# Delta-rule stage: f32 products replaced by products of f16 pairs, single buffers for the decayed blocks and decay rows

## The reference, cut to what matters

```python
def step(state, inp):
    q_t, k_t, v_t, g_t, b_t = inp
    state = state * jnp.exp(g_t)[..., None, None]
    kv_mem = jnp.einsum('bhkv,bhk->bhv', state, k_t)
    delta = (v_t - kv_mem) * b_t[..., None]
    state = state + k_t[..., None] * delta[..., None, :]
    out = jnp.einsum('bhkv,bhk->bhv', state, q_t)
    return (state, out)
```

## Time and profile before

| | before |
|---|---|
| median of 3 runs | 3533.2 us (3532.31 to 3538.77) |
| the profiled execution's own time | 3529.42 us |
| its span, first to last instruction | 3527.7 us |
| mean granted clock of PE over the span | 0.954 |
| PE, PEld busy | 3090.6 us (88%), 2170.7 us (62%) |
| DVE, ACT, POOL busy | 2636.8 us (75%), 2127.8 us (60%), 1516.7 us (43%) |
| first and last second-chunk cast (one for each unit) | 886.2 us, 3175.2 us |

### The profile page before, as it was taken

The page is one execution under the profiler, slowest core; times in us unless marked ns, Lnnn a source line. Parts: engine busy times, 40 slices in busy tenths (PEclk is TensorE's granted clock), DMA queues, the critical chain, the costliest instruction groups (busy, mean ns, idle before and its releaser), DMA issues. The chain is left out here.

```text
span 3527.7 us, 82159 instructions
## 1 busy us (share of the span) xinstructions
PE 3090.6 (88%) x29280; PEld 2170.7 (62%) x29280; DVE 2636.8 (75%) x4740; ACT 2127.8 (60%) x5446; POOL 1516.7 (43%) x1853
## 2 busy tenths in 40 slices
PE   6999788347999999999999999999999999983285
PEld 4666565235777676776767767677676777762142
DVE  3444389874888877888778887788877888776875
ACT  4444410135777777777777777777777777763553
POOL 1111177224555454555545555455554555530000
PEclk9999999778999999999999999999999999996698
DMA  4000011001101011010110101101011010101101
GB/s 191 13 13 1 9 39 42 24 21 46 37 20 38 20 34 42 20 38 20 38 38 20 38 20 42 34 20 38 20 44 33 20 37 20 44 8 63 80 1 48
DMA packets 43229, 120.67 MB, mean 34 GB/s; under 512 B 5824, under 2 KB 10048, under 8 KB 39488
## 3 DMA queue, kind: packets, MB, share of 16 engines
q1 hardware_dynamic: 42816, 115.30, 10.6%
HBM read 110.75 MB, written 4.54 MB: 33 GB/s over the span
## 5 line engine op out<-in xcount | busy, mean ns | idle before, releaser
L2020 DVE TENSOR_TENSOR delta_Pb<-delta_bank,delta_lev 128x512 f16<-128x512 f32 x448 | 311.2, 695 | 196.1 <-PE delta_bank L2350 194.6
L1590 POOL TENSOR_SCALAR_AFFINE_SELECT delta_LA<-delta_LA 128x512 f32<-128x512 f32 x128 | 81.2, 635 | 807.0 <-DVE delta_LA L2049 797.6
L2012 DVE SCALAR_TENSOR_TENSOR delta_F<-delta_bank,delta_cw,delta_F 128x510 f32<-128x510 f32 (+1 forms) x512 | 381.2, 745 | 62.4 <-ACT delta_far L1828 50.1
L2324 PE MATMUL delta_bank<-delta_xh,delta_qkvh 128*128 128x512 f16 x1024 | 390.6, 381 | 4.6 <-DVE delta_qkvl L1985 3.1
L2324 PE MATMUL delta_bank<-delta_xl,delta_qkvh 128*128 128x512 f16 x1024 | 390.4, 381 | 0.0
L2324 PE MATMUL delta_bank<-delta_xh,delta_qkvl 128*128 128x512 f16 x1024 | 390.3, 381 | 0.0
L1610 POOL TENSOR_TENSOR delta_F<-delta_F,delta_far 128x506 f32<-128x506 f32 x256 | 277.6, 1084 | 207.0 <-DVE delta_F L2012 207.0
L1822 ACT ACTIVATE delta_F<-delta_bank,delta_cw 128x512 f32<-128x512 f32 x256 | 178.1, 696 | 270.5 <-PE delta_bank L2324 270.2
L2037 DVE CAST delta_XT<-delta_bank 128x512 f16<-128x512 f32 x384 | 263.2, 686 | 78.0 <-PE delta_bank L2369 77.3
L2309 PE MATMUL delta_bank<-delta_zh,delta_xh 128*128 128x256 f16 x1024 | 279.0, 272 | 0.6 <-ACT delta_gz L1850 0.6
L2309 PE MATMUL delta_bank<-delta_zl,delta_xh 128*128 128x256 f16 x1024 | 278.8, 272 | 0.0
(11 more groups left out here) (352 smaller groups left out, 9302.3 us busy)
## 6 DMA issues: line engine op xcount, KB each, us to landing
delta_Gb<-g_rows SPq DMA_DIRECT2D x66, 512.0 KB, 5.4
delta_st_qkv<-in_Wqkv SPq DMA_DIRECT2D x17, 1024.0 KB, 8.7
conv_T<-filters SPq DMA_DIRECT2D x32, 256.0 KB, 3.1
delta_st_zo<-in_Wz SPq DMA_DIRECT2D x16, 512.0 KB, 9.3
delta_st_zo<-in_Wout SPq DMA_DIRECT2D x16, 512.0 KB, 6.4
ffn_ahead_W<-in_W SPq DMA_DIRECT2D x2, 4096.0 KB, 16.7
conv_ahead_C<-in_ctx_rev SPq DMA_DIRECT2D x1, 6144.0 KB, 26.5
attn_xt<-in_xT SPq DMA_DIRECT2D x8, 512.0 KB, 4.2
```

Source lines behind the costliest of these rows:

```text
L2012: ve.scalar_tensor_tensor(dst, src, cw_tap(i, 3 - lag), dst, ALU.mult, ALU.add)\
L2020: ve.tensor_tensor(left(Pb[:, lvl, :, :], lvl), comp(bank[5], lvl), bc(lev[:, lvl, :].rearrange("p (n s) -> p n s", s=1 << lvl), 1, 8), AL ...
L2324: ins = te.matmul(bk[:, :], ww[:, QKV[job], kc, :], xx[:, kc, tok:tok + 512], start=(m == 0), stop=(m == 11))
```

## The change

L00, L11, L10, A00, A10 and A11 now lie in one f32 buffer `LA` of 6 x 128 columns for each q. A00, A10, A11 and L10 are split into f16 pairs: the high parts by ACT (`split_high`, four copies of 128x512 in a turn), the low parts by POOL (`split_low`, four subtractions of 128x512). `Ah` and `Al` have two buffers by parity, `Bh` and `Bl` (L10) one. `W` is gone: the first answer stays in `W16`, now one for each chunk, and `refined` casts the correction to `Wl16`. Each of the sixteen f32 matmuls of a unit becomes three f16 ones (`split_product`). `decayed_j0` no longer waits for `o` of two units earlier, but for `ll` and `alo` of the unit before. `Gb` has one buffer, loaded three units ahead of unit 0 and not four. Two aliases of the prologue move to `gz`. The core of the diff:

```diff
-        Gb = sb("Gb", [P, 2, 2, 512])
+        Gb = sb("Gb", [P, 2, 512])
-        LA = sb("LA", [P, 2, 4, 2, 384])
+        LA = sb("LA", [P, 4, 768])
+        Ah, Al = sb("Ah", [P, 2, 3, 4, P], F16), sb("Al", [P, 2, 3, 4, P], F16)
+        Bh, Bl = sb("Bh", [P, 4, P], F16), sb("Bl", [P, 4, P], F16)
-        W, W16 = sb("W", [P, 2, 4, P]), sb("W16", [P, 4, P], F16)
+        W16, Wl16 = sb("W16", [P, 2, 4, P], F16), sb("Wl16", [P, 2, 4, P], F16)
+        L00, L10, A00, A10, A11 = 128, 256, 384, 512, 640
+        split_from = (A00, A10, A11, L10)
+        def split_to(n, u, part):
+            return (Bh, Bl)[part][:, :, :] if n == 3 else (Ah, Al)[part][:, u % 2, n, :, :]
...
@@ def turn of @block.sync @@
-                    if it.has(4):
-                        load_g(it.u(4), it.kh(4))
+                    if it.has(3):
+                        load_g(it.u(3), it.kh(3))
...
@@ def turn of @block.gpsimd @@
+                def split_low(n):
+                    after("ahi", n + 1, 1)
+                    if n < 3:
+                        after("o", 2, -1)
+                    else:
+                        after("sv", 4, 0)
+                    by_sequencer()
+                    gp.tensor_tensor(split_to(n, it.u(1), 1), LA[:, :, split_from[n]:split_from[n] + P],
+                                     split_to(n, it.u(1), 0), ALU.subtract).then_inc(g["alo"].sem, 1)
+
                 if it.has(1):
+                    split_low(0)
                     after("v", 2, 1)
                     after("sv", 1, 0)
                     by_sequencer()
                     gp.tensor_copy(V16[:, :, :], values[it.u(1) % 2][:, :, 0, :]).then_inc(g["v16"].sem, 1)
                 if it.has(2):
                     conv_far("v1")
+                if it.has(1):
+                    split_low(1)
...
                 if it.has(1):
                     low_L(0)
                     low_L(1)
+                    split_low(2)
+                    split_low(3)
...
@@ def turn of @block.scalar @@
+                def split_high(n):
+
+                    if not it.has(1):
+                        return
+                    after("la", 8, 1)
+                    if n < 3:
+                        after("o", 2, -1)
+                    else:
+                        after("sv", 4, 0)
+                    sc.activation(split_to(n, it.u(1), 0), LA[:, :, split_from[n]:split_from[n] + P], ACT.Copy)\
+                        .then_inc(g["ahi"].sem, 1)
...
                 gate(0)
+                split_high(0)
+                split_high(1)
+                split_high(2)
                 conv_tap("v1")
                 level_x(1, 1)
                 next_qkv(0)
                 next_qkv(1)
+                split_high(3)
                 first_answer(1)
...
@@ def turn of @block.vector @@
-                    after("o", 2, -1)
+                    after("ll", 2, 0)
+                    after("alo", 4, 0)
...
                     after("sv", 3 + 4 * k, 0)
-                    after("u0", k + 1, 0)
-                    ve.tensor_tensor(W[:, k, :, :], W16[:, :, :], heads(bank[2]), ALU.add).then_inc(g["w"].sem, 1)
+                    ve.tensor_copy(flat(Wl16[:, k, :, :]), bank[2][:, :]).then_inc(g["w"].sem, 1)
...
@@ def turn of @block.tensor @@
+                def split_product(out, q, n, k, start, stop):
+                    high, low = (split_to(n, it.u(0), part)[:, q, :] for part in (0, 1))
+                    te.matmul(out, high, W16[:, k, q, :], start=start, stop=False)
+                    te.matmul(out, high, Wl16[:, k, q, :], start=False, stop=False)
+                    return te.matmul(out, low, W16[:, k, q, :], start=False, stop=stop)
...
-                            last = te.matmul(out, LA[:, it.u(0) % 2, q, 0, P:2 * P], W[:, 0, q, :], start=True,
-                                             stop=True)
+                            last = split_product(out, q, 3, 0, True, True)
...
-                        te.matmul(out, LA[:, it.u(0) % 2, q, 1, P:2 * P], W[:, 0, q, :], start=True, stop=False)
-                        last = te.matmul(out, LA[:, it.u(0) % 2, q, 1, 2 * P:3 * P], W[:, 1, q, :], start=False,
-                                         stop=True)
+                        split_product(out, q, 1, 0, True, False)
+                        last = split_product(out, q, 2, 1, False, True)
```

More of the change, by code:

```diff
@@ L1380, in delta_stage @@
             sv=7, u0=2, r=2, w=2, t16=1, t2=1, o=2,
-            so=8, rr=1, lr=1, rn0=1, rn=3, ogs=8, og=2, ct=2, ch=2, cl=2,
+            ahi=4, alo=4, so=8, rr=1, lr=1, rn0=1, rn=3, ogs=8, og=2, ct=2, ch=2, cl=2,
         ).items():
             g[name] = counter(name, per)
-        g_load = [counter(f"g_load{i}", 1, 16) for i in range(2)]
+        g_load = counter("g_load", 1, 16)
         w_load = {n: counter(f"load_{n}", 1, 16) for n in ("qkv", "z", "o", "c")}
@@ L1396, in delta_stage @@
         pro_g = counter("pro_gstore", 0, 16)
-        wba = LA[:, 1, 0, :, :].rearrange("p a b -> p (a b)")[:, 0:256].rearrange("p (k c) -> p k c", k=KC)
+        wba = LA[:, 0, 0:256].rearrange("p (k c) -> p k c", k=KC)
         wbah = Pb[:, 0, 0:2, :].rearrange("p a b -> p (a b)").rearrange("p (k c) -> p k c", k=KC)
         wbal = Pb[:, 0, 2:4, :].rearrange("p a b -> p (a b)").rearrange("p (k c) -> p k c", k=KC)
-        dtr = LA[:, 1, 1, 0, 0:32]
-        nal = LA[:, 1, 1, 0, 32:64]
-        al0 = LA[:, 1, 1, 0, 64:96]
+        dtr = LA[:, 1, 0:32]
+        nal = LA[:, 1, 32:64]
+        al0 = LA[:, 1, 64:96]
         full = lambda t: t.rearrange("p a b -> p (a b)").rearrange("p (a b) -> p a b", b=NVH)
@@ L1410, in delta_stage @@
         gg = full(V[:, 1, 4:8, :])
-        lnb = full(W[:, 0, :, :])
+        lnb = gz[:, 0:2, :].rearrange("p a b -> p (a b)").rearrange("p (a b) -> p a b", b=NVH)
         tri = EL[:, 0, 0:128]
-        GT = W[0:32, :, :, :].rearrange("p a b c -> p (a b c)")
+        GT = gz[0:32, :, :].rearrange("p a b -> p (a b)")
         def left(t, lvl):
@@ L1513, in _ @@
             turns(nc, ENG.SP, turn)
-            for par in range(2):
-                sp.wait_ge(g_load[par].sem, g_load[par].at(NU // 2 + 1))
+            sp.wait_ge(g_load.sem, g_load.at(NU + 1))
             sp.wait_ge(w_load["qkv"].sem, w_load["qkv"].at(NKH + 1))
@@ L1586, in unit_diagonal @@
                     par = it.u(1) % 2
-                    diag = LA[:, par, :, 0, 256 * c:256 * c + P]
+                    diag = LA[:, :, L00 - P * c:L00 - P * c + P]
                     after("la", 4 + 4 * c, 1)
@@ L1793, in first_answer @@
                     after("sv", 1 + 4 * k, 0)
-                    sc.activation(flat(W16[:, :, :]), bank[2][:, :], ACT.Copy).then_inc(g["u0"].sem, 1)
+                    sc.activation(flat(W16[:, k, :, :]), bank[2][:, :], ACT.Copy).then_inc(g["u0"].sem, 1)
+                def split_high(n):
[8 more added lines that the diff above has]
+                        .then_inc(g["ahi"].sem, 1)
                 def token_major(b_):
@@ L2467, in times_L @@
                     if blk == 1:
+                        after("u0", 1, 0)
                         after("w", 1, 0)
+                        after("alo", 4, 0)
                     else:
@@ L2474, in times_L @@
                         if blk == 1:
-                            last = te.matmul(out, LA[:, it.u(0) % 2, q, 0, P:2 * P], W[:, 0, q, :], start=True,
-                                             stop=True)
-                        else:
-                            te.matmul(out, Lt16[:, it.u(0) % 2, 2 * q + k, :], W16[:, q, :], start=True, stop=False)
-                            last = te.matmul(out, Ll16[:, 2 * q + k, :], W16[:, q, :], start=False, stop=True)
+                            last = split_product(out, q, 3, 0, True, True)
+                        else:
+                            te.matmul(out, Lt16[:, it.u(0) % 2, 2 * q + k, :], W16[:, k, q, :], start=True, stop=False)
+                            last = te.matmul(out, Ll16[:, 2 * q + k, :], W16[:, k, q, :], start=False, stop=True)
                     last.then_inc(g["sv"].sem, 1)
@@ L2486, in output_first @@
                     for q in range(4):
-                        last = te.matmul(bank[OUT[0]][:, q * P:(q + 1) * P], LA[:, it.u(0) % 2, q, 1, 0:P],
-                                         W[:, 0, q, :], start=True, stop=True)
+                        last = split_product(bank[OUT[0]][:, q * P:(q + 1) * P], q, 0, 0, True, True)
                     last.then_inc(g["o"].sem, 1)
```

18 lines of the change are left out of this document (9 added, 9 removed).

## The result

The changed kernel takes 3510.4 us, the median of four runs (3504.9 to 3513.3), beside 3535.7 (3532.3 to 3538.8, four runs) for the kernel before: ratio 0.9931, interval 0.9912 to 0.9949. It is faster by 25 us. The forecast was 42 faster, 3491 us; 3510 lies in the stated range, 3458 to 3529, but outside the 3480 to 3502 of the case that was held likeliest.

A forecast was written before the change was run, and what follows sets the result against it. PE was taken to bound the delta stage (1978 of 2000 us busy). Plain turns -48 and loaded turns +6 gave -42 us: 3529.4 to 3487, forecast as a 3491 us median, range 3458 to 3529.

The forecast's parts named there:

- the case that was held likeliest: Whole kernel: the main forecast, 3491 us for a median, own range 3480 to 3502, chance 0.50.
- The products' lengths: PE's L10 W0, A00 W0 and `output_second` go from 0.97, 0.95, 1.87 to 0.67, 0.67, 1.34 us.
- L10 W0 and the wait behind it: PE keeps 0.30 us of this product, plus 0.18 waiting for DVE's f16 cast, which beats POOL by 0.24.
- rival 1: PE's wait for w2 doesn't bind, so plain turns are 1.3 us shorter: 70 us saved, 3463; chance 0.11.
- A00 W0's 0.28 lost to the wait for w2: PE's shorter A00 W0 gains nothing: it waits 0.4 us for DVE's `add_out(0, -1)` instead of about 0.1.
- ACT's and POOL's additions cost nothing in plain turns: ACT's three copies (1.84 us) fit a 1.95 us hole; POOL's 4.6 us of subtractions is covered.
- DVE never waited for `alo`: `decayed_j0(0)`'s new wait on DVE has over two us left; DVE waiting there would make the forecast wrong.
- stretched DVE steps in plain turns: Sign against the forecast: DVE's other steps with two inputs in SBUF stretched in plain turns; no size given.
- Loaded turns later at `level_a(3, 1)`: In 16 loaded turns w2 starts 0.6 to 1.2 us later; each turn +0.4 (+0.1 to +0.7), together +6 us.
- rival 2: DVE's cast loses the port to POOL in 16 to 32 plain turns, worth 0 each: 3507 to 3523; chance 0.20.
- rival 3: DVE's cast loses the port everywhere; plain turns give 0.0, loaded ones lose 11 us: 3544; chance 0.11.
- the sum itself: 48 plain turns at 1.01 us saved, 16 loaded at 0.4 added: -48 + 6 = -42 us.

The follow-up runs named there:

- experiment 6: Changed kernel with 60 turns in one iteration (no jump), plus five overwritten f16 matmuls in `output_first`: 3468.3 us, 1.4 more than without them.
- experiment 4: Changed kernel with its loop body lengthened to 60 turns in one iteration, so no jump back: 3466.9 us, ratio 0.9817 to the kernel before.
- experiment 5: Kernel before with 60 turns in one iteration, so no jump back: 3514.0 us, ratio 0.9953 to the kernel before.
- experiment 1: Changed kernel with 32 f16 matmuls (64 instructions) put ahead of PE's loop, results overwritten: 3491.7 us, one run.
- experiment 2: Changed kernel with 64 f16 matmuls (128 instructions) put ahead of PE's loop, results overwritten: 3490.3 us, one run.
- experiment 10: Changed kernel with 96 matmuls (192 instructions) put ahead of PE's loop: 3495.7 us, one run.
- experiment 7: Changed kernel without jumps, with DVE's `add_out(0, -1)` moved ahead of `level_p(3, 1)` and `refined(1)`: 3451.0 us, ratio 0.9772 to the kernel before.
- experiment 11: Changed kernel without jumps, DVE's `add_out(0, -1)` early and POOL's `split_low(0)` behind its v1 convolution: 3448.2 us, ratio 0.9755 to the kernel before.

## Why the prediction was right and wrong

- **The products' lengths** (0.67, 0.67, 1.34): right, to the hundredth.
- **L10 W0 and the wait behind it, 0.30 + 0.18:** right in kind, too small. In plain turns the cast won the port with the margin worked out, ended 0.29 behind POOL, and the wait went. But it was longer than its bracket. The earlier trace rows show 0.18 at 1724.15; the start before it was 1723.57, and eight such matmuls take 0.24, so PE stood for 0.34. The bracket counts from the modelled end of a matmul. With 0.34 a plain turn loses 1.17, and 1.20 were measured. That is a term of the sum too small by 48 x 0.16 = 8 us, and the sign named for rival 1, plain turns shorter by 1.3, was nearly met by it (1.20), though rival 1's reason is wrong.
- **A00 W0's 0.28 lost to the wait for w2:** right (0.38 of waiting in each plain turn; experiment 6). Rival 1 falls.
- **ACT's and POOL's additions cost nothing in plain turns:** right. ACT's three copies fit in the hole and 0.39 of it is left:

```profile
1710.77 1.68 ACT L1826 ACTIVATE delta_Ah<-delta_LA 128x512 f16<-128x512 f32 x3
1712.83 0.69 ACT L1855 ACTIVATE delta_F<-delta_bank,delta_cw 128x512 f32<-128x512 f32 x1 [0.39 <-PE delta_bank L2362]
```

DVE never waited for `alo`. `low_L` began at 1719.31 without a gap behind `split_low(1)`, and the z weights' low parts on DVE went from 1.28 to 2.79 us for two beside POOL, with nobody waiting for them. The prediction had named stretched DVE steps in plain turns as a sign against it; here they came, in one plain turn of four, and cost nothing.
- **Loaded turns later at `level_a(3, 1)`:** right, +0.3 against +0.4, by fours of turns (3 x 1.20 - 3.3). Job w2 starts 8.87 us behind the cast, where it was 8.07 in loaded turns of before (8.40 in the one of the earlier trace rows, which has the jump): 0.80 later, inside the 0.6 to 1.2 forecast. The chain is the one foretold, POOL to ACT to PE:

```profile
1787.51 1.17 POOL L1662 TENSOR_TENSOR delta_Al<-delta_LA,delta_Ah 128x512 f16<-128x512 f32 x1
1788.61 0.62 POOL L1670 CAST delta_V<-delta_V 128x512 f16<-128x512 f32 x1
1789.17 1.53 POOL L1616 TENSOR_TENSOR delta_F<-delta_F,delta_far 128x506 f32<-128x506 f32 x1
```

```profile
1790.74 0.63 ACT L1870 ACTIVATE delta_F<-delta_F 128x512 f32<-128x512 f32 x1 [1.53 <-POOL delta_F L1616]
...
1791.80 0.58 ACT L1808 ACTIVATE delta_Xi<-delta_bank 128x512 f16<-128x512 f32 x1
```

```profile
1792.43 0.41 PE L2388 MATMUL delta_bank<-delta_Xi,delta_Lt 128*128 128x64 f16 x8 [1.11 <-ACT delta_Xi L1808]
```

- **Rivals 2 and 3, the port lost:** it was lost in four turns of 64, those behind the jumps, where rival 2 had it in 16 to 32; the median of the casts is 0.54 us. Such a turn was worth 0.1 us (36.07 to 35.96), near rival 2's 0. The time, 3510, stands in rival 2's own range, 3507 to 3523, but the lost casts are 4 x 0.9 = 4 us of it; most of the way there came from the jumps. That the time is in the stated range is owed in part to luck: the range was wide for rivals 1 and 2, and had nothing in it for what happened.
- **What failed is the sum itself.** It was made of plain and loaded turns, 48 and 16, and had no term for the four turns in which PE jumps back. What the runs show in its place is +7.2 us each, +29 us. Without the jumps the sum of -42 would have stood beside -49 (from the fours of turns) or -47 (experiments 4 and 5). The diff doesn't touch the jump, but it changes the number of PE's instructions in each turn, and with it the loop's place and length (which of the two counted here was not separated: the place alone moved the idle time by 2.2 us in the one kernel and by 3.4 in the other, and no place tried brought the kernel after down to 1.3); and PE's waits of before have four gaps of 1.1 to 1.6 us marked `issue`, which the forecast didn't read.

That the idle time is the fetching of instructions is argued from the times in the traces, not shown by an experiment. The profile has DMA queues of kind "instruction". On one of them, q8, packets of 16 KB come every 14 us or so. The DMA view of after from 1800.5 to 1800.8 has one:

```profile
q8 instruction: 1, 0.02, 28.2%
```

It starts at 1800.64, and 28.2% of 16 engines' 0.3 us is 1.35 us, so it landed at 1802.0; PE goes on at 1803.39, 1.4 later. It is so at every idle time over half a us at or behind a jump, in all kernels with jumps, 34 in number: the last packet of q8 landed 1.2 to 2.4 us before PE's next instruction. The length goes with when that packet starts. In the kernel after it starts 2.5 to 3.3 us after PE has stopped (5.3 us idle), in the kernel before 1.4 to 1.5 ahead of the stop (1.3 idle), and with the loop moved (experiments 1 and 2, and the first idle time of 10) it starts 0.2 to 0.8 ahead (1.9 to 3.3 idle). Three idle times without a jump have such a packet too, of 0.5 us in experiment 4 and of 1.2 in 7 and 11. That q8 is PE's own queue is inferred from this. One `issue` of 0.7 us near the stage's end, in all changed kernels, has no such packet and stays open, as does which places are good.

## What to carry to other kernels

Where a hand-scheduled loop holds hundreds of instructions to a turn, read the idle time marked "issue" at its jump back before and after every change, and give the jump a term of its own: here it was 2.0 us before and 9.2 after, and the difference took more than half of what the change's own work brought (29 of 49). Compare two versions without jumps, or at several places of the loop, before judging an edit of a fraction of a per cent; unrolling, where it can be afforded, took 43 us off here. Read PE's waits from start to start, not from the bracket.

## What the runs showed of the hardware

- PE's idle time at the loop's jump ranged from 1.1 to 5.6 us in these kernels, and changed with the loop's place in the stream: 64 instructions more ahead of it brought it from 5.3 to 3.1 in one kernel and from 1.3 to 4.7 (in two parts) in the other.
- In an idle time of 5.3 us PE's granted clock fell to 0.50 and stayed there for the first 4.5 us of work behind it, which cost 2.2 us more; behind 1.2 us of idle time it was 1.00. Between the two it varied: of the four jumps of experiment 1 (3.0 to 3.3 us idle) the clock was 0.50 for a stretch behind three, whose turns took 41.8 to 42.1 us, and 1.00 behind the fourth, whose turn took 40.2.
- A DVE cast that waits for POOL ends 0.28 to 0.29 us behind POOL's instruction, and goes ahead of what POOL issues next, also where POOL's queue is full without a gap (1714.45 to 1724.27). Where POOL's next subtraction and the cast start together (1830.74), POOL's runs first and the cast takes 1.44 us; in experiment 1, issued 0.16 ahead of it, the cast takes 0.48. The Trainium skill, SBUF — State Buffer, section "Who interferes with whom", has the mutual lock and that whoever issues first gets it; the trace agrees.
- Three f16 matmuls of 128 columns take 0.17 us where one in f32 takes 0.24.
